# A transposed input loaded and normalised on GpSimd in place of TensorE transposes, in a 16-batch attention and FFN kernel

## The reference

```python
xn = _layernorm(x)                       # per token, over D = 256
s = attention_block(xn, ...)             # 16 heads of 16
g = silu(fp4_ffn(xn, w_gate, w_up, w_down))
return x + s * g
```

## Time and profile before

| what | value |
|---|---|
| times of 3 runs | 1918.35, 1924.22, 1926.29 us; median 1924.22 |
| span of the profiled execution | 1916.1 us, first to last instruction; the median of the runs is 8.1 us above it |
| busy: TensorE, weight loads | 1822.3 us (95%), 1311.7 us (68%) |
| busy: VectorE, ScalarE, GpSimd | 1590.4 us (83%), 930.2 us (49%), 1095.4 us (57%) |
| mean granted TensorE clock | 0.991 of full speed |
| chain that ended last, by engine | TensorE 50%, VectorE 26%, "issue" 12%, GpSimd 4%, DMA 3%, ScalarE 3% |
| DMA | 166.69 MB, mean 87 GB/s |

### The profile page before, as it was taken

The page is one execution under the profiler, slowest core; times in us unless marked ns, Lnnn a source line. Parts: engine busy times, 40 slices in busy tenths (PEclk is TensorE's granted clock), DMA queues, the critical chain, the costliest instruction groups (busy, mean ns, idle before and its releaser), DMA issues.

```text
span 1916.1 us, 37547 instructions
## 1 busy us (share of the span) xinstructions
PE 1822.3 (95%) x12803; PEld 1311.7 (68%) x12803; DVE 1590.4 (83%) x5143; ACT 930.2 (49%) x1939; POOL 1095.4 (57%) x797
## 2 busy tenths in 40 slices
PE   7888999999999999999999999999999999999987
PEld 3335677777767767676776767677776767677766
DVE  6788899788888989888888978888897988888863
ACT  3635454544546354544635454453645445463542
POOL 2446657465556647464665746565664756466562
PEclk8999999999999999999999999999999999999999
DMA  5534233232322233232223323233222333322211
GB/s 156 165 96 114 64 91 83 75 110 75 99 75 79 76 82 115 75 90 73 91 74 93 93 75 110 64 102 79 83 77 75 110 84 91 75 85 74 61 57 34
DMA packets 138646, 166.69 MB, mean 87 GB/s; under 512 B 19757, under 2 KB 100654, under 8 KB 138452
## 3 DMA queue, kind: packets, MB, share of 16 engines
q1 hardware_dynamic: 138458, 164.30, 30.5%
HBM read 127.85 MB, written 36.41 MB: 86 GB/s over the span
## 4 chain that ended last, share of the span: by engine, by line
PE 50%; DVE 26%; issue 12%; POOL 4%; DMA 3%; ACT 3%; SPq 2%; DVEq 0%; POOLq 0%; ACTq 0%
PE ps L760 8%; PE ps L769 7%; PE ps L701 7%; PE ps L718 4%; DVE Pr L1067 3%; PE ps L624 3%; PE ps L597 3%; PE ps L733 3%; PE ps L658 3%; PE ps L674 2%; DVE nmax L1037 2%; POOL slot L1215 2%; PE ps L654 2%; DMA Tz<-kernel_rows 2%; DVE st L958 2%
## 5 line engine op out<-in xcount | busy, mean ns | idle before, releaser
L1176 POOL TENSOR_TENSOR Pr<-Pr,Tz 128x768 f32<-128x768 f32 (+2 forms) x384 | 477.6, 1273 | 233.8 <-ACT Pr L833 230.0
L1037 DVE CUSTOM_DVE_ANT_0 ps<-ps,future 128x512 f32<-128x512 f32 (+3 forms) x1024 | 474.5, 516 | 52.9 <-issue 51.8
L833 ACT ACTIVATE Pr<-ps 128x384 f32<-128x384 f32 x512 | 243.1, 489 | 345.2 <-PE ps L658 343.9
L760 PE MATMUL ps<-catT,w 128*128 128x256 f32 x1024 | 237.8, 380 | 0.7 <-ACT catT L896 0.7
L769 PE MATMUL ps<-w,gT 128*128 128x256 f32 x1024 | 232.9, 381 | 0.9 <-ACT gT L913 0.9
L624 PE MATMUL ps<-KS,QS 108*128 108x512 bf16 (+3 forms) x1024 | 215.0, 300 | 17.9 <-DVE nmax L1037 13.2
L822 ACT ACTIVATE ps<-ps 128x512 f32<-128x512 f32 x256 | 150.5, 588 | 137.7 <-PE ps L654 136.1
L1067 DVE SCALAR_TENSOR_TENSOR Pr<-ps,Tz 128x512 f32<-128x512 f32 x256 | 175.3, 685 | 46.2 <-ACT ps L822 41.0
L769 PEld LDWEIGHTS ps<-w,gT 128*128 128x128 f32 x1024 | 190.8, 190 | 25.7 <-ACT gT L913 1.3
L760 PEld LDWEIGHTS ps<-catT,w 128*128 128x128 f32 x1024 | 189.6, 190 | 26.2 <-ACT catT L896 0.9
L718 PE MATMUL ps<-wdT,hqT 128*128 128x256 f32 x768 | 179.5, 383 | 0.7 <-ACT hqT L872 0.7
(11 more groups left out here) (239 smaller groups left out, 3270.0 us busy)
## 6 DMA issues: line engine op xcount, KB each, us to landing
Tz<-kernel_rows SPq DMA_DIRECT2D x256, 256.0 KB, 3.6
KS<-k_parts SPq DMA_DIRECT2D x32, 384.0 KB
QS<-q_parts SPq DMA_DIRECT2D x64, 192.0 KB
hY<-in_x SPq DMA_DIRECT2D x19, 512.0 KB, 5.1
xn<-in_x SPq DMA_DIRECT2D x17, 512.0 KB, 3.8
out<-y SPq DMA_DIRECT2D x15, 512.0 KB, 2.9
q_parts<-q_sp SPq DMA_DIRECT2D x16, 384.0 KB, 3.0
k_parts<-k_sp SPq DMA_DIRECT2D x16, 384.0 KB, 2.4
```

Source lines behind the costliest of these rows:

```text
L760: ins = mm(dst[:, i * n:(i + 1) * n], w1[:, c, f * P:(f + 1) * P], catT[:, c, hf * n:(hf + 1) * n], start=c == 0, stop=c == KD - 1)
L833: inc(af(Pr[:, p % 4, e, at:at + wd], src[:, 0:wd], ACT.Exp), "a_exp")
L1037: ins = v.tensor_tensor_reduce(o, o, future[:, S - n:S], -1.0, 3e38, ALU.add, ALU.min, nmax[:, 2 * pl + e, it:it + 1])
L1176: ins = g.tensor_tensor(a, a, Tz[:, p % 2, :, P * j:P * j + PAST[j]], ALU.mult)
```

## The change

The input is given to the kernel a second time, transposed to [16, 256, 512] (`x_t`; made on the host, like the other rearranged inputs). In each middle batch a new step `xt` on SyncE loads it straight into `xnT`, and loads the means and the 1/std of the 512 tokens, each row repeated on all 128 partitions, into `q_r` and `k_r`, which are free then. A new step `xt` on GpSimd subtracts and multiplies. `proj` and `v` wait for it. The steps `xT` on TensorE and ScalarE go from the middle batches; batches 0 and 1 are still transposed on TensorE in the head. A new prologue step `stat` transposes `mean_all` and `rstd_all`, copies them to rows (in a piece of `xnb`) and writes them to DRAM; `first:xnb` waits for that.

All the step lists are laid out anew, in the head and the end too. `psum_plan` now hands out banks in one sequence over all batches, where it used one plan for every middle batch.

The middle lists:

```diff
     mid=dict(
         sync="""
-            T.0 load.1 T.1 T.2 xload T.3 mio.1 T.4 splitio T.5 load.0 T.6 T.7 fin mio.0
+            T.0 load.1 T.1 xload T.2 xt T.3 T.4 mio.1 splitio T.5 load.0 T.6 T.7 fin mio.0
         """,
         gpsimd="""
-            ln1 mul.0 lnb1 xnb mul.1 hq.0 mul.2 hr.0 projm.0 mul.3 hq.1 projm.1 hr.1 projm.2 xq xr mul.4 hq.2 mul.5
-            ln2 hr.2 fin mul.6 hq.3 mul.7 hr.3
+            ln1 xnb lnb1 mul.0 mul.1 hq.0 xt mul.2 hr.0 hq.1 projm.0 projm.1 projm.2 mul.3 xq mul.4 hr.1 hq.2 hr.2 ln2
+            mul.5 xr mul.6 fin hq.3 mul.7 hr.3
         """,
         vector="""
-            out.0 out.1 ln1 muld.0.0 silu.0.0 lnc1 silu.0.1 muld.0.1 mx.1.0.0 lnb1 mx.1.0.1 mx.1.0.2 muld.1.0 mx.1.0.3
-            silu.1.0 mx.1.0.4 mx.1.1.0 muld.1.1 mx.1.1.1 mx.1.1.2 mx.1.1.3 mx.1.1.4 muld.2.0 mx.1.2.0 mx.1.2.1 hq.0
-            mx.1.2.2 mx.1.2.3 norm mx.1.2.4 mx.1.3.0 muld.2.1 mx.1.3.1 mx.1.3.2 mx.1.3.3 mx.1.3.4 muld.3.0 mfin.1 hr.0
-            silu.1.1 f2.0 muld.3.1 proj.0 hq.1 f2.1 ctxt.0 proj.1 proj.2 muld.4.0 hr.1 xq muld.4.1 xr xr2 silu.2.0
-            muld.5.0 silu.2.1 hq.2 v.0 v.1 muld.5.1 f2.2 hr.2 mx.0.0.0 mx.0.0.1 f2.3 ln2 mx.0.0.2 mx.0.0.3 muld.6.0
-            silu.3.0 ctxt.1 muld.6.1 lnc2 lnb2 mx.0.0.4 mx.0.1.0 dn.0 silu.3.1 muld.7.0 mx.0.1.1 mx.0.1.2 mx.0.1.3
-            mx.0.1.4 hq.3 muld.7.1 mx.0.2.0 mx.0.2.1 mx.0.2.2 mx.0.2.3 mx.0.2.4 dn.1 ctxt.2 hr.3 mx.0.3.0 mx.0.3.1
-            dn.2 mx.0.3.2 mx.0.3.3 mx.0.3.4 mfin.0 ctxt.3 dn.3
+            out.0 out.1 ln1 muld.0.0 lnc1 silu.0.0 lnb1 muld.0.1 silu.0.1 mx.1.0.0 mx.1.0.1 mx.1.0.2 muld.1.0 mx.1.0.3
+            silu.1.0 mx.1.0.4 mx.1.1.0 muld.1.1 mx.1.1.1 mx.1.1.2 norm mx.1.1.3 mx.1.1.4 muld.2.0 mx.1.2.0 mx.1.2.1 hq.0
+            mx.1.2.2 mx.1.2.3 mx.1.2.4 mx.1.3.0 muld.2.1 mx.1.3.1 mx.1.3.2 mx.1.3.3 mx.1.3.4 mfin.1 muld.3.0 silu.1.1
+            hr.0 f2.0 muld.3.1 proj.0 hq.1 proj.1 proj.2 f2.1 ctxt.0 muld.4.0 xq muld.4.1 hr.1 xr silu.2.0 muld.5.0 xr2
+            silu.2.1 v.0 hq.2 mx.0.0.0 muld.5.1 hr.2 f2.2 f2.3 mx.0.0.1 mx.0.0.2 ln2 muld.6.0 mx.0.0.3 lnc2 mx.0.0.4
+            muld.6.1 v.1 mx.0.1.0 lnb2 silu.3.0 mx.0.1.1 muld.7.0 mx.0.1.2 dn.0 mx.0.1.3 mx.0.1.4 silu.3.1 muld.7.1 hq.3
+            ctxt.1 mx.0.2.0 mx.0.2.1 mx.0.2.2 dn.1 mx.0.2.3 mx.0.2.4 ctxt.2 hr.3 dn.2 mx.0.3.0 mx.0.3.1 mx.0.3.2
+            mx.0.3.3 mx.0.3.4 mfin.0 ctxt.3 dn.3
         """,
         tensor="""
-            cT out.0 out.1 sc.0.0 gu.0.0 sc.0.1 gu.0.1 sc.0.2 sc.0.3 mx.1.0.0 mx.1.0.1 sc.0.4 gu.1.0 sc.0.5 mx.1.0.2
-            sc.1.0 hT sc.1.1 mx.1.0.3 sc.1.2 sc.1.3 mx.1.0.4 mx.1.1.0 sc.1.4 f1.0.0 mx.1.1.1 mx.1.1.2 f1.0.1 sc.1.5
-            sc.2.0 mx.1.1.3 mx.1.1.4 f1.0.2 mx.1.2.0 mx.1.2.1 f1.0.3 mx.1.2.2 mx.1.2.3 sc.2.1 sc.2.2 pv.0 sc.2.3
-            mx.1.2.4 mx.1.3.0 gu.1.1 mx.1.3.1 sc.2.4 xT.0 sc.2.5 sc.3.0 mx.1.3.2 xT.1 sc.3.1 ctxt.0 mx.1.3.3 mx.1.3.4
-            f2.0 mT.1 sc.3.2 sc.3.3 proj.0 sc.3.4 proj.1 proj.2 sc.3.5 f2.1 sc.4.0 sc.4.1 f1.1.0 tr.0.0 f1.1.1 f1.1.2
-            f1.1.3 sc.4.2 sc.4.3 gu.2.0 gu.2.1 sc.4.4 sc.4.5 v.0 sc.5.0 sc.5.1 v.1 f2.2 tr.0.1 sc.5.2 sc.5.3 f2.3
-            sc.5.4 sc.5.5 mx.0.0.0 mx.0.0.1 pv.1 sc.6.0 mx.0.0.2 mx.0.0.3 gu.3.0 sc.6.1 ctxt.1 sc.6.2 sc.6.3 mx.0.0.4
-            mx.0.1.0 sc.6.4 dn.0 sc.6.5 sc.7.0 gu.3.1 mx.0.1.1 pv.2 mx.0.1.2 sc.7.1 tr.1.0 mx.0.1.3 tr.1.1 mx.0.1.4
-            tr.2.0 sc.7.2 sc.7.3 mx.0.2.0 dn.1 sc.7.4 mx.0.2.1 sc.7.5 tr.2.1 mx.0.2.2 ctxt.2 mx.0.2.3 mx.0.2.4 dn.2
-            mx.0.3.0 mx.0.3.1 pv.3 mx.0.3.2 mx.0.3.3 xqT mx.0.3.4 tr.3.0 tr.3.1 ctxt.3 mT.0 dn.3
+            cT out.0 out.1 sc.0.0 gu.0.0 sc.0.1 gu.0.1 sc.0.2 sc.0.3 sc.0.4 mx.1.0.0 gu.1.0 sc.0.5 mx.1.0.1 sc.1.0
+            mx.1.0.2 sc.1.1 hT mx.1.0.3 mx.1.0.4 sc.1.2 sc.1.3 mx.1.1.0 sc.1.4 f1.0.0 mx.1.1.1 mx.1.1.2 f1.0.1 sc.1.5
+            mx.1.1.3 sc.2.0 mx.1.1.4 f1.0.2 mx.1.2.0 sc.2.1 mx.1.2.1 f1.0.3 sc.2.2 mx.1.2.2 mx.1.2.3 pv.0 sc.2.3
+            mx.1.2.4 mx.1.3.0 gu.1.1 mx.1.3.1 sc.2.4 mx.1.3.2 sc.2.5 ctxt.0 sc.3.0 sc.3.1 mx.1.3.3 mx.1.3.4 f2.0 sc.3.2
+            sc.3.3 mT.1 proj.0 proj.1 proj.2 sc.3.4 sc.3.5 f2.1 sc.4.0 sc.4.1 f1.1.0 sc.4.2 sc.4.3 f1.1.1 sc.4.4 f1.1.2
+            f1.1.3 tr.0.0 sc.4.5 gu.2.0 sc.5.0 sc.5.1 gu.2.1 tr.0.1 v.0 sc.5.2 f2.2 sc.5.3 mx.0.0.0 f2.3 mx.0.0.1 sc.5.4
+            mx.0.0.2 sc.5.5 pv.1 sc.6.0 mx.0.0.3 sc.6.1 gu.3.0 mx.0.0.4 sc.6.2 sc.6.3 v.1 tr.1.0 mx.0.1.0 sc.6.4 sc.6.5
+            dn.0 sc.7.0 tr.1.1 sc.7.1 mx.0.1.1 mx.0.1.2 gu.3.1 mx.0.1.3 sc.7.2 mx.0.1.4 sc.7.3 ctxt.1 pv.2 mx.0.2.0
+            mx.0.2.1 sc.7.4 sc.7.5 dn.1 mx.0.2.2 tr.2.0 tr.2.1 mx.0.2.3 ctxt.2 mx.0.2.4 dn.2 mx.0.3.0 mx.0.3.1 pv.3
+            mx.0.3.2 mx.0.3.3 xqT mx.0.3.4 tr.3.0 tr.3.1 ctxt.3 mT.0 dn.3
         """,
         scalar="""
-            cT sc.0.0 vcopy silu.0.0 sc.0.1 silu.0.1 sc.0.2 sc.0.3 sc.0.4 sc.0.5 sc.1.0 hT silu.1.0 sc.1.1 sc.1.2
-            sc.1.3 sc.1.4 sc.1.5 sc.2.0 f1.0.0 f1.0.1 f1.0.2 f1.0.3 sc.2.1 sc.2.2 sc.2.3 ctxe.0 sc.2.4 xT.0 sc.2.5
-            silu.1.1 xT.1 sc.3.0 sc.3.1 mT.1 sc.3.2 sc.3.3 proj.0 projm.0 sc.3.4 proj.1 sc.3.5 proj.2 sc.4.0 sc.4.1
-            projm.1 projm.2 tr.0.0 f1.1.0 f1.1.1 f1.1.2 f1.1.3 sc.4.2 sc.4.3 sc.4.4 sc.4.5 silu.2.0 gscopy sc.5.0
-            sc.5.1 silu.2.1 sc.5.2 sc.5.3 sc.5.4 sc.5.5 tr.0.1 sc.6.0 ctxe.1 silu.3.0 sc.6.1 sc.6.2 sc.6.3 sc.6.4
-            sc.6.5 sc.7.0 dn.0 silu.3.1 ctxe.2 sc.7.1 tr.1.0 tr.1.1 sc.7.2 sc.7.3 sc.7.4 sc.7.5 tr.2.0 dn.1 tr.2.1
-            dn.2 ctxe.3 xqT tr.3.0 tr.3.1 mT.0 dn.3
+            cT sc.0.0 sc.0.1 silu.0.0 sc.0.2 silu.0.1 sc.0.3 sc.0.4 sc.0.5 silu.1.0 sc.1.0 hT sc.1.1 sc.1.2 sc.1.3 vcopy
+            sc.1.4 gscopy sc.1.5 sc.2.0 f1.0.0 f1.0.1 f1.0.2 f1.0.3 sc.2.1 sc.2.2 sc.2.3 ctxe.0 sc.2.4 sc.2.5 silu.1.1
+            sc.3.0 sc.3.1 sc.3.2 mT.1 sc.3.3 proj.0 sc.3.4 proj.1 sc.3.5 projm.0 proj.2 projm.1 projm.2 sc.4.0 sc.4.1
+            sc.4.2 sc.4.3 sc.4.4 f1.1.0 f1.1.1 f1.1.2 f1.1.3 sc.4.5 tr.0.0 silu.2.0 sc.5.0 tr.0.1 silu.2.1 sc.5.1 sc.5.2
+            sc.5.3 sc.5.4 sc.5.5 sc.6.0 sc.6.1 ctxe.1 sc.6.2 silu.3.0 sc.6.3 sc.6.4 sc.6.5 sc.7.0 tr.1.0 dn.0 tr.1.1
+            sc.7.1 silu.3.1 sc.7.2 sc.7.3 sc.7.4 sc.7.5 ctxe.2 dn.1 tr.2.0 tr.2.1 dn.2 ctxe.3 xqT tr.3.0 tr.3.1 mT.0
+            dn.3
         """,
     ),
```

```diff
-... last:pv.3 last:ctxt.2 last:ctxt.3 tail:cT tail:out.0 tail:out.1 last:tr.3.0 last:tr.3.1 last:dn.3 tail:hT.0
+... last:pv.3 last:ctxt.2 last:ctxt.3 last:tr.3.0 last:tr.3.1 tail:cT tail:out.0 last:dn.3 tail:out.1 tail:hT.0
```

The rest of the diff, without the bank plan's body:

```diff
-                g_fin=1).items():
+                g_fin=1, g_xc=1, g_xt=1).items():
             E[name] = event(name, per)
         v_mul = [event(f"v_mul{e}", PAIRS) for e in range(2)]
         d_x = event("d_x", 1, 16)
+        d_xt = event("d_xt", 3, 16)
         d_T = [[event(f"d_T{i}{e}", PAIRS // 2, 16) for e in range(2)] for i in range(2)]
         d_split = event("d_split", 6 + 2 * T, 16)
         NLOAD = 6
@@ -464,13 +455,12 @@
             elif k == "dn":
                 E["v_gs"].wait(eng, b, u[1])
 
-        def bank_for(ring, released, eng, u, which, b):
+        def bank_for(ring, released, eng, u, b):
 
             place, before = plans[ring]
-            if (which, u) in before:
-                earlier, ago = before[which, u]
-                released(eng, earlier, b + ago)
-            return ps[:, place[which, u], :]
+            if (b, u) in before:
+                released(eng, *before[b, u])
+            return ps[:, place[b, u], :]
 
         def half_batch(half, b):
 
@@ -487,6 +477,15 @@
                     E["g_xs"].wait(sp, b)
                     E["g_xnb"].wait(sp, b)
                     sp.dma_start(xn[:], x_b[b + 1]).then_inc(d_x.sem, 16)
+                elif k == "xt":
+                    E["pe_proj"].wait(sp, b)
+                    E["pe_v"].wait(sp, b)
+                    sp.dma_start(xnT[:], xt_b[b + 1]).then_inc(d_xt.sem, 16)
+                    E["g_lo"].wait(sp, b, 1)
+                    if b == 1:
+                        sp.wait_ge(L["stat"], 32)
+                    for i, r in enumerate((q_r, k_r)):
+                        sp.dma_start(r[:], stat_d[i, b + 1:b + 2, :].to_broadcast([P, S])).then_inc(d_xt.sem, 16)
                 elif k == "splitio":
                     d_load[0].wait(sp, b)
                     d_load[1].wait(sp, b)
@@ -589,7 +588,10 @@
                 elif k == "proj":
                     if which == "pro" and s[1] == 0:
                         pe.wait_ge(L["w_proj"], 16 * len(loads["w_proj"]))
-                    E["a_xT"].wait(pe, b + 1)
+                    if which == "mid":
+                        E["g_xt"].wait(pe, b - 1)
+                    else:
+                        E["a_xT"].wait(pe, b + 1)
                     dst = b_bank(s)
                     wt = (cq, ck, bw)[s[1]]
                     for c in range(KD):
@@ -1189,9 +1194,15 @@
                     E["v_xq"].wait(pool, b + 1)
                     wide = lambda a: a.unsqueeze(2).to_broadcast([P, T * D // BLK, BLK])
```

(43 more changed lines are left out.)

264 lines of the change are left out of this document (127 added, 137 removed).

## The result

The changed kernel takes 2046.28 us (median of four runs), the kernel before 1922.62 beside it: ratio 1.0646, 95% interval 1.0624 to 1.0668. The prediction said 1904.8 us, 1889 to 1922, with 0.13 for slower: the sign is wrong, and the time lies outside the range.

A forecast was written before the change was run, and what follows sets the result against it. TensorE's work plus some 2.7 us of small waits was taken to bound middle batches. -1.10 us per batch times 14 is -15.4; with -2 for head and -2 for end, 1924.2 becomes 1904.8 us, range 1889 to 1922.

The forecast's parts named there:

- GpSimd against VectorE: Middle batch, `xnb` beside `lnc1` and `mul.5` beside `lnc2`: GpSimd mostly waits, costing 0.2 us per batch.
- The bounds 0 to 2.37: Middle batch, `lnc1` beside `xnb`: 0 if GpSimd waits for all four instructions, 2.37 us if VectorE waits.
- Rival A: Middle batches: VectorE is held at `lnc1` and `lnc2`, +2.3 us per batch, 1952 us in all; chance 0.14.
- The slack of 2.2 us at `hT`: Middle batch: VectorE's `lnb1` placed earlier was to give `hT` 2.2 us to spare.
- the terms for the work itself: Middle batch: `xt` behind `hq.0`, two passes of 2.37 us, fits idle time; loads taken as 7 us; cost 0.
- `projm.2`: Middle batch: placed before `mul.3` on GpSimd, it ends at about 1054 instead of 1059.31 + 0.44; no gain counted.
- The waits at `hT` and `tr.3`: Middle batch, TensorE: both idle times go by reordered steps, 0.34 and 0.29 us per batch.
- The 0.89 us for the transposes: Middle batch, TensorE: removing `xT.0` and `xT.1` saves 0.89 us of pure work per batch, counting in full.
- Head: forecast -2: Head: new order and `basis` loads moved back give -2 us, bounds 4.37 us won or lost.
- End: forecast -2: End: `dn.3` behind `out.0` and `tr.3` ahead of `cT` give -2 us, bounds 0 and -3.
- rival C: Middle batches: all TensorE waits but 0.74 us go; 1879 us at best, 1887 for three quarters; chance 0.13.
- 0.9 us less per batch: Middle batches: the faster side of the likeliest case's range, 1895 to 1914 us, with the head's bounds.

The follow-up runs named there:

- the old head lists: Changed kernel with the middle and head lists of the kernel before, `stat` put in, GpSimd's `xt` behind `hq.0` and waiting for `norm`: 1920.46 us, ratio 0.9984.
- the run with one meeting in the kernel before: Kernel before, without `xt`, with GpSimd's `xnb` moved directly behind `ln1` in the middle batches: 2010.62 us, ratio 1.0461.
- old middle lists with `xt`: Changed kernel with the middle-batch lists of the kernel before, transposes and their copies taken out, `xt` behind `hq.0`: 1956.85 us, ratio 1.0179.

## Why the prediction was wrong

The step that failed is "GpSimd against VectorE", which took 0.2 us per batch, "near the lower bound, because the row that exists shows GpSimd waiting". The changed kernel shows 10.7 us more on these four steps of VectorE. TensorE has 8.1 us of new waits for VectorE and 1.4 more at the lower clock; less some 1.1 that was won, this is the 8.4. Runs show 4.6 of it (`lnc2` and `lnb2` freed). The other 3.8, laid here to `lnc1` and `xr2`, are argued from the timelines, as each run that freed `lnc1` brought another meeting.
- The bounds 0 to 2.37 were those of one hold at `lnc1`. It measured 2.1 there, near the upper end: `xnb` is one instruction, and there was one hold. But where GpSimd has one instruction behind the other, the price is one of them for each VectorE instruction of the step, not one for each step: 4.6 us at `lnc2` (four against four), 3.0 at `lnb2` (four against the three of `mul.6`), and 1.0 at `xr2`. The last two meetings, with `mul.6` and `mul.4`, weren't on paper at all.
- Rival A had the mechanism, and a quarter of the size (+2.3 us against +8.4), as it counted holds by step and no clock. Its chance of 0.14 was argued from one row in which GpSimd waits. Rows of the kernel before show the other direction, for another form, and were overlooked. In the head, beside `wm.2.0` of GpSimd (128.22 to 131.53), a `tensor_scalar` that takes 0.69 us in the middle batches of the changed kernel took 3.18.

```profile
128.91 3.18 DVE L936 TENSOR_SCALAR hY<-hY 128x1024 f32<-128x1024 f32 x1
...
1048.23 1.40 DVE L930 TENSOR_SCALAR sc_h<-sc_h 128x44 f32<-128x44 f32 x1
...
1070.44 0.77 DVE L926 TENSOR_SCALAR sc_h<-sc_h 128x44 f32<-128x44 f32 x1
```

  The other two rows stand in a middle batch, beside `mul.3` and `mul.4`; such a step takes 0.19 us with no GpSimd work beside it (1029.23 us). So the kernel before already paid for such meetings.

- The slack of 2.2 us at `hT` was there (no wait before `hT`), but the delay fell on `gu.1` and `mx` ahead of it.

Right were the terms for the work itself. `xt` takes 2.35 and 2.36 us behind `hq.0` with no wait for a DMA before it; the 512 KB landed in 4.8 us. `projm.2` ends 50.7 us after the start of `out` (forecast 50.9), and the idle time before `mul.2` is gone. The waits at `hT` and `tr.3` went. The 0.89 us for the transposes are 0.76 of TensorE's busy time; that they count in full was wrong, 0.2 us was left of them even with no meeting.

Head: forecast -2, measured +10.3. The timelines of the changed kernel show the same mechanism there. `norm` of batch 1 takes 8.62 us instead of 1.37, its four parts 1.89 to 2.96 us long, beside four GpSimd instructions of 1.80 to 2.80 us, and TensorE waits 11.70 us for it; its longest wait in the head before was 4.37:

```profile
143.58 8.62 DVE L1000 TENSOR_SCALAR xn<-xn,mean_all,rstd_all 128x256 f32<-128x256 f32 x4
```

```profile
143.62 1.80 POOL L1401 TENSOR_TENSOR gT<-gT,slot 128x768 f32<-128x768 f32 x1 [6.66 <-DVE gT L1488]
145.38 1.85 POOL L1401 TENSOR_TENSOR gT<-gT,hqT 128x768 f32<-128x768 f32 x1
147.31 2.80 POOL L1403 TENSOR_TENSOR gT<-gT,gs_old 128x1536 f32<-128x1536 f32 x1
150.07 1.98 POOL L1196 TENSOR_TENSOR catT<-catT,sc_x 128x1024 f32<-128x1024 f32 x1
```

```profile
152.25 1.12 PE L586 MATMUL ps<-ident,xn 128*128 128x128 f32 x4 [11.70 <-DVE xn L1000]
```

How much of the 10.3 us this is stays open: with the old head lists `norm` took 1.37 us again and the head was still 9 us longer than before. And executions differ in the head by nearly as much. In the run with one meeting in the kernel before, all the head lists are those of the kernel before, and yet its first `out` starts 7.3 us later:

```profile
234.22 3.72 PE L733 MATMUL ps<-ow,catT 128*128 128x256 f32 x16 [0.74 <-ACT catT L891]
241.50 3.72 PE L736 MATMUL ps<-ow,catT 128*128 128x256 f32 x16 [0.74 <-ACT catT L894]
```

So the profiled execution of the kernel before had a short head, and the 10.3 us of one pair of executions are not the price of the new head. The medians put it nearer to the 7.5 us that the old head lists won. Either way the forecast of -2 was wrong. End: forecast -2. The same end lists took 146.8 us here and 144.0 in the run with the old head, against 146.1, so its sign isn't settled.

Two sums of the prediction are off without bearing on the outcome: three quarters of rival C give 1890 us, not 1887, and 0.9 us less per batch reaches down to 1892, not 1895.

## What to carry to other kernels

Before GpSimd work is moved or added, write down for each VectorE instruction with two SBUF inputs, or a `tensor_scalar` from SBUF to SBUF, which GpSimd instruction runs beside it, and charge one GpSimd instruction for each VectorE instruction that meets one, not one for each step: one for `lnc1` beside the single `xnb`, four for `lnc2` beside four. Look for the price in the trace at hand, by the longest against the usual duration of one form, also in stages that the change doesn't touch. Where two engines meet by chance, a wait that keeps the second one out can be cheaper than the overlap: it won 4.6 us per batch here at `mul.5`, and 29 us in all at `xt`.

## What the runs showed of the hardware

- A VectorE instruction with two SBUF inputs is held until the GpSimd instruction that runs beside it ends, and the engines take turns: 1.89, 1.49, 0.94 and 2.15 us instead of 0.48 beside GpSimd instructions of 1.82, 1.45, 0.90 and 2.11.
- A `tensor_scalar` from SBUF to SBUF is held too: a `norm` of four parts takes 1.38, about 3.4 or 5.5 us, for none, one or two passes of `xt` beside it, and with four GpSimd instructions beside it 8.62; one of 128x44 takes 1.40 instead of 0.19.
- `muld`, which has one input in PSUM, isn't held: it takes 0.68 us beside `mul.4`, as it does on average over the batch.
- TensorE at the full clock idled 4.39 us and was then granted 0.74 over 6.5 us; behind idle times of 3.46 us (one meeting in the kernel before) and 2.76 us (old middle lists with `xt`) it was granted 0.50. In the first two, a matmul group took 1.4 and 0.9 us longer for it (`dn.0`, `hT`), so such a wait costs more than its length.
